# A hybrid convolution-attention block on one core: keys streamed once, the narrow band masked on GpSimd, products of ones on TensorE

## What is computed

```
# x: (8, 128, 16, 16)
attn = softmax(theta(x)^T phi(x), axis=1);  y = attn @ g(x);  x = w_mask y + x     # per image
t = tokens(x)                                                                      # (8, 256, 128)
# attention over 256 tokens, 8 heads of 16, in two bands
scores = q k^T * 16 ** -0.5
for ws in (9, 17):                       # half widths 4 and 8
    masked = where(|i - j| <= ws // 2, scores, -max)
    out += softmax(masked) @ v
t = t + (out / 2) @ proj_w.T + proj_b    # q, k, v from layernorm(t)
t = t + fp8(layernorm(t)) @ fp8(kernel) + bias
```

## Time and profile before

| | |
|---|---|
| Median of 3 runs | 106.75 us (106.66 to 107.17) |
| The profiled execution | 106.25 us, of which the span from first to last instruction is 104.5 us |
| PE busy | 87.1 us (83%), 1825 instructions |
| PE weight loads | 65.7 us (63%) |
| DVE busy | 77.4 us (74%), 283 instructions |
| ACT busy | 63.5 us (61%) |
| POOL busy | 56.3 us (54%) |
| Mean granted TensorE clock | 0.907 |

### The profile page before, as it was taken

One profiled execution on the slowest core, in us unless ns is written; L12 is line 12 of the kernel. 1 busy time (PEld: TensorE's weight loads), 2 busy tenths in 40 slices (PEclk: granted clock), 3 DMA queues, 4 the chain that ended last, 5 costly groups with the idle time before them and its releaser, 6 DMA issues.

```text
span 104.5 us, 4371 instructions
## 1 busy us (share of the span) xinstructions
PE 87.1 (83%) x1825; PEld 65.7 (63%) x1825; DVE 77.4 (74%) x283; ACT 63.5 (61%) x174; POOL 56.3 (54%) x118
## 2 busy tenths in 40 slices
PE   0799786999997999999999999989979757777260
PEld 0485474877775888797688788658849536444120
DVE  0011528199999999999999999999999895736221
ACT  1524556679584649974967956994996644162520
POOL 6810202057593944939799296789649464630300
PEclk9999999999999999999999999999999975555555
DMA  0725400000000000000010010000101010010101
GB/s 22 205 49 170 157 0 0 6 0 0 9 3 0 9 0 6 0 6 0 6 56 0 0 56 3 6 6 0 50 6 56 0 55 5 6 50 0 50 0 50
DMA packets 3971, 2.90 MB, mean 28 GB/s; under 512 B 944, under 2 KB 3952, under 8 KB 3952
## 3 DMA queue, kind: packets, MB, share of 16 engines
q1 hardware_dynamic: 3728, 2.56, 7.8%
q10 hardware_dynamic: 224, 0.07, 0.3%
HBM read 1.57 MB, written 1.05 MB: 25 GB/s over the span
## 4 chain that ended last, share of the span: by engine, by line
PE 55%; DVE 27%; POOL 8%; issue 3%; ACT 2%; DMA 2%; DVEq 0%
PE bank L309 10%; PE bank L323 5%; PE bank L331 5%; PE bank L300 4%; PE bank L257 4%; PE bank L266 4%; PE bank L252 4%; PE bank L274 3%; DVE row_max L791 3%; PE bank L293 3%; DVE z_sb L780 3%; PE bank L289 3%; DMA phi_w<-in_L_conv_w_phi_dram 2%; PE bank L272 2%; PE bank L294 2%
## 5 line engine op out<-in xcount | busy, mean ns | idle before, releaser
L309 PE MATMUL bank<-k_pad,q_four 64*64 64x64 f32 x512 | 17.4, 220 | 1.2 <-ACT q_four L548 1.1
L309 PEld LDWEIGHTS bank<-k_pad,q_four 64*64 64x64 f32 x512 | 15.8, 135 | 3.1 <-ACT q_four L548 1.8
L1122 POOL TENSOR_TENSOR prob<-expd,row_inv 128x256 f32<-128x256 f32 x16 | 9.9, 616 | 9.8 <-DVE row_inv L806 9.8
L323 PEld LDWEIGHTS bank<-prob_t,v_win 32*32 32x32 f32 x1024 | 10.9, 110 | 5.2 <-issue 2.7
L1116 POOL TENSOR_TENSOR diff<-narrow,row_max 128x192 f32<-128x192 f32 x16 | 8.2, 514 | 10.3 <-DVE row_max L791 10.3
L323 PE MATMUL bank<-prob_t,v_win 32*32 32x32 f32 x1024 | 12.7, 199 | 1.0 <-DVE prob_t L810 1.0
L548 ACT ACTIVATE q_four<-bank,four_mask 128x256 f32<-128x256 f32 x32 | 12.6, 483 | 0.0
L791 DVE TENSOR_REDUCE row_max<-bank 128x16 f32<-128x512 f32 x16 | 10.7, 671 | 2.1 <-ACT narrow L555 2.1
L1097 POOL TENSOR_TENSOR rstd<-ve,minus_half 128x2 f32<-128x2 f32 x8 | 5.6, 701 | 11.9 <-DVE ve L774 11.8
L555 ACT COPY narrow<-bank 128x192 f32<-128x192 f32 x16 | 5.1, 318 | 8.0 <-PE bank L309 8.0
L1129 POOL TENSOR_TENSOR prob<-prob,narrow_prob 128x192 f32<-128x192 f32 x16 | 9.5, 594 | 0.5
(11 more groups left out here) (116 smaller groups left out, 213.2 us busy)
## 6 DMA issues: line engine op xcount, KB each, us to landing
x_all<-in_x_dram SPq DMA_DIRECT2D x8, 128.0 KB, 3.8
out_dram<-out_all SPq DMA_DIRECT2D x8, 128.0 KB, 1.7
qkv_rows<-in_L_attn_qkv_w_dram SPq DMA_DIRECT2D x1, 192.0 KB, 2.6
proj_rows<-in_L_attn_proj_w_dram SPq DMA_DIRECT2D x1, 64.0 KB, 2.7
ffn_k<-in_L_ffn_kernel_dram SPq DMA_DIRECT2D x1, 64.0 KB, 2.2
proj_bias<-in_L_attn_proj_b_dram SPq DMA_DIRECT2D x1, 64.0 KB, 4.4
theta_w<-in_L_conv_w_theta_dram SPq DMA_DIRECT2D x1, 32.0 KB, 2.0
phi_w<-in_L_conv_w_phi_dram ACTq DMA_DIRECT2D x1, 32.0 KB, 2.4
```

Of the source, the lines that this page charges most:

```text
L309: last = mm(ps_scores[g][q, w, :, :], q_four[q, u % SLOTS, g * WB + w, :, :].rearrange("p e q -> p (e q)"), k_pad[q, u % SLOTS, at:at + KW ...
L323: last = mm(ps_pv[q, at:at + QUAD], v_win[q, u % SLOTS, g * WB + w, :], prob_t[q, u % SLOTS, g, w, :], start=True, stop=True)
L1122: p.tensor_tensor(prob[:, u % SLOTS, g], wide_part(expd, u, g), row_inv[:, u % SLOTS, g, 0].unsqueeze(2).to_broadcast([C, WB, KW]), ALU.mult)
```

## The change

It has five parts.

- The keys are streamed once: the score bank holds only the wide kind (256 columns instead of 512), the mask product has 256 columns, each score product 32.
- The narrow kind is made from the wide one: `copy_narrow` copies the inner 24 columns to a new tile `near`, `mask_narrow` on POOL adds a mask to it, and a new `narrow_max` on DVE takes its maximum; `band_max` reads 256 columns of PSUM. The narrow mask is spread over the 128 partitions once, by one small product (`spread_narrow`) and one copy.
- At the opening DVE fills a tile with ones, and PE makes 12 products of 256 columns in bfloat16 with it, ahead of its first product.
- In the last stretch nine groups of such products, 59 in all, stand in PE's list ahead of calls that wait. No one reads what they write.
- The lists of all four engines are written out in a new order.

```
+        warm_rows = sb("warm_rows", [C, TOK], BF16)
+            def keep_warm(at, count):
+                for _ in range(count):
+                    mm(bank[at][:, 0:TOK], warm_rows[:, 0:C], warm_rows[:, :], start=True, stop=True)
+
+            def begin_warm(count):
+                pe.wait_ge(warm_made, 1)
+                keep_warm(7, count)
+            def spread_narrow():
+                pe.wait_ge(masks_made, 1)
+                pe.wait_ge(weight_done, 3)
+                mm(bank[6][:, C:C + NW], query_sel[:, :, :].rearrange("p h q -> p (h q)"), narrow_rows[:, :],
+                   start=True, stop=True).then_inc(weight_mm, 1)
...
-                mm(bank[4 + g][:, :], query_sel[:, :, :].rearrange("p h q -> p (h q)"),
-                   key_mask[:, g:g + WB, :, :].rearrange("p w k n -> p (w k n)"), start=True, stop=False)
+                mm(bank[4 + g][:, 0:WB * KW], query_sel[:, :, :].rearrange("p h q -> p (h q)"),
+                   key_mask[:, g:g + WB, :].rearrange("p w n -> p (w n)"), start=True, stop=False)
...
-                        last = mm(ps_scores[g][q, w, :, :],
+                        last = mm(ps_scores[g][q, w, :],
                                   q_four[q, u % SLOTS, g * WB + w, :, :].rearrange("p e q -> p (e q)"),
-                                  k_pad[q, u % SLOTS, at:at + KW].unsqueeze(1).to_broadcast([SIDE, KINDS, KW]),
+                                  k_pad[q, u % SLOTS, at:at + KW],
...
+            begin_warm(12)
             fold_bilinear()
...
-                nc.scalar.copy(narrow[:, u % SLOTS, g], ps_scores[g][:, :, 1, INSET:INSET + NW]).then_inc(narrow_kept[g], 1)
+                nc.scalar.copy(near[:, u % SLOTS, g], ps_scores[g][:, :, INSET:INSET + NW]).then_inc(narrow_kept[g], 1)
...
-                v.tensor_reduce(row_max[:, u % SLOTS, g], ps_scores[g], AX.X, ALU.max).then_inc(max_done[g], 1)
+                v.tensor_reduce(row_max[:, u % SLOTS, g, 0], ps_scores[g], AX.X, ALU.max).then_inc(max_done[g], 1)
...
+            def narrow_max(u, g):
+                dve.wait_ge(narrow_made[g], u + 1)
+                v.tensor_reduce(row_max[:, u % SLOTS, g, 1], narrow[:, u % SLOTS, g], AX.X, ALU.max).then_inc(nmax_made[g], 1)
...
+            def mask_narrow(u, g):
+                if u == 0:
+                    pool.wait_ge(mask_kept, 1)
+                pool.wait_ge(narrow_kept[g], u + 1)
+                p.tensor_tensor(narrow[:, u % SLOTS, g], near[:, u % SLOTS, g],
+                                narrow_mask[:, :].unsqueeze(1).to_broadcast([C, WB, NW]), ALU.add).then_inc(narrow_made[g], 1)
...
             def subtract_narrow(u, g):
-                pool.wait_ge(max_done[g], u + 1)
+                pool.wait_ge(nmax_made[g], u + 1)
```

More of the change, by code:

```diff
@@ L151, in hybrid_block_kernel @@
         ps_q, ps_k = bank[3][:, 0:TOK], bank[3][:, TOK:2 * TOK]
-        ps_scores = [bank[4 + g][:, :].rearrange("p (w k n) -> p w k n", w=WB, k=KINDS) for g in range(BANKS)]
+        ps_scores = [bank[4 + g][:, 0:WB * KW].rearrange("p (w n) -> p w n", w=WB) for g in range(BANKS)]
         ps_pv, ps_proj = bank[6][:, :], bank[6][:, 0:TOK]
@@ L436, in _ @@
             turn_z2(1)
[L437 to L438 removed]
+            weigh_values(3, 0)
             project_kq(5)
[L440 to L441 removed]
             lay_mask(5, 0)
[L443 removed]
             feed_forward(1)
+            weigh_values(3, 1)
+            turn_t2(2)
             lay_mask(5, 1)
[L446 removed]
+            scores(5, 0)
+            project_g(7)
             scores(5, 1)
[L448 removed]
@@ L898, in _ @@
             row_inverse(1, 1)
+            window_values(2)
             band_max(2, 0)
-            norm_first(3)
-            pick_odd(0)
             turn_probs(1, 0)
-            window_values(2)
             residual(0)
+            band_max(2, 1)
+            stats_second(0)
+            narrow_max(2, 0)
+            subtract_max(2, 0)
+            stats_first(4)
+            column_max(5)
+            aggregate_first(4)
+            aggregate_second(0)
+            narrow_max(2, 1)
+            variance_first(4)
@@ L930, in _ @@
-            band_max(3, 1)
-            residual(1)
-            subtract_max(3, 1)
-            band_max(3, 0)
-            stats_first(5)
-            stats_second(1)
+            stats_first(5)
+            band_max(3, 1)
+            aggregate_second(1)
+            column_inverse(6)
+            band_max(3, 0)
+            subtract_max(3, 1)
+            quantise_half(0)
+            turn_probs(2, 1)
+            narrow_max(3, 0)
+            aggregate_first(5)
             subtract_max(3, 0)
-            turn_probs(2, 1)
@@ L972, in _ @@
-            pick_odd(3)
-            norm_first(6)
+            column_inverse(7)
             window_values(5)
-            column_inverse(7)
             turn_probs(4, 0)
-            band_max(5, 1)
-            residual(3)
-            band_max(5, 0)
-            subtract_max(5, 1)
-            subtract_max(5, 0)
-            turn_probs(4, 1)
-            stats_first(7)
+            residual(3)
+            narrow_max(5, 0)
+            band_max(5, 0)
+            stats_first(7)
+            subtract_max(5, 0)
@@ L993, in _ @@
             row_sums(5, 1)
-            pick_odd(4)
+            result(2)
             row_inverse(5, 1)
-            norm_first(7)
-            window_values(6)
-            result(2)
+            residual(4)
+            turn_probs(5, 0)
+            band_max(6, 1)
             band_max(6, 0)
-            band_max(6, 1)
-            turn_probs(5, 0)
+            subtract_max(6, 0)
+            turn_probs(5, 1)
+            narrow_max(6, 0)
+            quantise_tiny(3)
             subtract_max(6, 1)
-            residual(4)
@@ L1004, in _ @@
-            subtract_max(6, 0)
             stats_second(4)
-            quantise_tiny(3)
-            turn_probs(5, 1)
+            quantise_half(3)
+            aggregate_second(4)
+            narrow_max(6, 1)
+            variance_second(4)
+            result(3)
             row_sums(6, 0)
-            quantise_half(3)
+            pick_odd(5)
             row_inverse(6, 0)
             row_sums(6, 1)
-            aggregate_second(4)
             row_inverse(6, 1)
-            variance_second(4)
```

438 lines of the change are left out of this document (243 added, 195 removed).

## The result

The changed kernel takes 103.59 us (median of 4 runs, 103.46 to 106.99), the kernel before 106.85 (4 runs, 106.66 to 107.17); the ratio is 0.969, with a 95% interval of 0.966 to 0.972. The median is inside the stated range and 1.2 us above the predicted 102.4. The profiled execution takes 103.52 us with a span of 101.8. The fourth run left no trace; its mean granted clock of 0.983 says that its clock also fell somewhere behind the rise.

What follows compares the result with a forecast made beforehand. PE and DVE were taken as full together, PE deciding to 69 us, then DVE, then one chain at half clock. Terms −0.7 −0.8 −1.7 −1.0 = −4.2 us from 106.25 gave 102.05, stated as 102.4; eight in ten from 100.7 to 105.3.

Steps and rivals of the forecast that it cites:

- Scores, 0: PE's score products: halving streamed columns gains 0, as the 64-column weight load sets the pace; bounds 0 and 8 us.
- rival 4: The scores do halve, capped by DVE's remaining idle time: 1.3 us more gained, 101.1 us; chance 8%.
- Mask product, −1.0: PE's mask product loses 256 columns, 0.11 us each of 16 times; 1.0 us in reach where PE decides.
- Middle as a whole, −0.7: Middle stretch: −1.0 mask product, +0.1 `spread_narrow`, +0.2 DVE gives −0.7 us; range −2.0 to +1.5.
- DVE, +0.2: Two maxima on DVE replace one at 0.56 to 0.60 against 0.61 us; +0.2 us taken, at most 1.6 in all.
- POOL, 0: 16 new `mask_narrow` on POOL, 8.2 to 9.5 us, and a longer narrow path, hidden by other units' work: cost 0.
- rival 2: The longer narrow path stalls DVE, half the units waiting 0.6 us each: 2.4 us come back, 104.8 us; chance 17%.
- Opening, −0.8: Twelve products raise PE's clock well before 10 us: 1.4 us won, 0.6 lost; bounds +0.6 and −1.6.
- rival 3: The opening's products don't bring the clock sooner: +0.6 in place of −0.8 us, 103.8 us; chance 12%.
- Drain, clock, −1.7: Products of ones hold PE at full clock in the drain, shortening the last chain by 1.7 us.
- Drain, order, −1.0: New order for the last unit: 0.7 and 0.6 us won, 0.3 off for stalls; bounds 0 and −2.0.
- Rival 1: The higher clock is lost in the drain despite the products: 1.7 us gain becomes 3.2 loss, 107.3 us; chance 8%.

Runs made afterwards that it cites:

- both sets: The kernel before with 12 products of ones at the opening and 50 late ones, nothing else; six runs from 103.78 to 106.32 us, ratio 0.977.
- narrow loads: The changed kernel with 32 instead of 64 weight columns in seven of eight score windows, half the heads' scores left out there; 102.65 and 103.14 us.
- the kernel with one exponential: The changed kernel with one subtraction and exponential for both bands, narrow probabilities cut out by a mask on POOL, lists otherwise unchanged; 125.84 us, ratio 1.165.

## Why the prediction was right, and where its sum was off

The forecast was faster by 4.2 us in the profiled execution; 2.7 came, within the range. The direction and the two clocks were right as mechanisms; every term but the two zeros was mis-sized, the order of the drain most. Step by step:

- *Scores, 0*: right, and shown from both sides: twice the streamed columns cost 0.02 us a unit, half the loaded columns bring the products of one half of the array from some 62 to 33 ns. The rule of the Trainium skill's page "TensorE: Matmul & The Clock Gate" (section "LDWEIGHTS (loading the stationary operand)") held against the view that streamed columns set the time, and rival 4 is out.
- *Mask product, −1.0*: some 0.6 to 0.75. At the start of the last bank's scores the new kernel is 0.80 us ahead, counted from the first scores (60.23 against 61.03 us), and with the wide mask product put back it is 0.06 ahead (60.97). So this relief of PE arrived, and the rest of the band and the order changed nothing up to there.
- *Middle as a whole, −0.7*: −0.10. What is lost is lost behind that point: from the start of the last bank's scores to the end of its subtraction pass 6.06 us before and 6.76 now. In the kernel before `project(5)` stands ahead of `scores(7, 1)` in PE's list (79.75 us in the earlier trace rows); now it stands behind, and DVE waits for it:

```profile
80.29 1.15 PE L309 MATMUL bank<-k_pad,q_four 64*64 64x64 f32 x32
```

```profile
78.08 1.12 PE L331 MATMUL bank<-k_pad,q_four 64*64 64x32 f32 x32
79.14 0.71 PE L353 MATMUL bank<-proj_t,att_t 128*128 128x128 f32 x4
79.95 0.42 DVE L867 TENSOR_TENSOR t_sb<-bank,tb_all 128x256 f32<-128x256 f32 x1 [0.67 <-PE bank L353]
```

The wait of 0.67 us is about what is lost, but no run moved that one call, so it is the likely cause, not shown. Taking the masking out (0.17) or three other residuals behind ready calls (0.21) shortens only what lies ahead: from the last bank's scores on it stays 6.76 us in both.
- *DVE, +0.2*: not seen. DVE's busy time fell from 77.4 to 75.6 us; in a full queue the two maxima take 0.32 and 0.24 us of the chain, against 0.61 for the one.
- *POOL, 0* was right, and rival 2 is out, though POOL has 15 of 16 us in one stretch. Full is not the same as deciding. From 31 to 69 us it is at 29.1 of 38 us, 76% and not the 86% of the forecast. The sign that was to refute the forecast, DVE waiting for `narrow`, did appear, once and for 0.31 us.
- *Opening, −0.8*: −1.41, of which 1.33 come with the products alone. The sum took 1.4 us won and 0.6 lost; PE began its first real product at 3.92 instead of 3.22 us, so 0.7 was lost and 2.1 won, since the clock was up before the first product of 256 columns. What was not foreseen is that it is a draw: rival 3 happens in part of the executions, and then the scores start 1.3 us later than in the kernel before, where it had 0.6, and 2.6 us later than in a good execution.
- *Drain, clock, −1.7*: −1.15, by the products alone in the old order.
- *Drain, order, −1.0*: 0. The drain is 14.82 us with the new order and 14.85 with the old.

The last two can be taken apart with the chains of the three kernels, unit 7, bank 1 (us):

| | before | late products, old order | changed |
|---|---|---|---|
| last subtraction's end to `scale_probs` | 3.29 | 3.14 | 2.44 |
| to `project` | 4.54 | 4.52 | 4.13 |
| to `residual` | 1.33 | 0.82 | 1.73 |
| to the last result's end | 6.84 | 6.37 | 6.52 |
| sum | 16.00 | 14.85 | 14.82 |

The first two columns are the clock. The projection gave 0.51 of the forecast's 0.61. Behind the residual 0.47 came where 0.75 was forecast: of the feed-forward only some 0.2 is on the chain, as its second product waits for ACT's copy, and the first of the two transposes gave nothing, as POOL's `rstd_second` takes as long beside it (2.85 us from the residual to `norm_second` before, 2.82 with the products). The 0.3 for the last values did not come at all (4.54 to 4.52): there too the chain goes through POOL and ACT, not through PE.

The last two columns are the order. Up to the projection it won 0.70 and 0.39 us, the 1.0 of the forecast. Then 0.91 went again at `residual(7)`: it stands behind `quantise_tiny(6)` in DVE's list, which waits 1.45 us for a transpose (92.80), while its own input is there from 92.12. Three products of ones stand in that chain too, from 92.12 to 92.44; the transpose's input is there at 92.27, so they cost 0.2 us where the forecast had 0. I took turns that a call gives up as time won, without following the calls that stand behind it to the end.

Of the 2.7 us, the products bring 2.5 (1.33 and 1.15) in executions in which both work, the band and the order some 0.2.

That the time lies in the range is in part luck. The opening's 0.6 us more stands against 2.1 us less in the other terms. And the median is that of a good draw: three of four executions had the short opening, where the same twelve products gave a short time in two of four and two of six executions of the old order. With an opening as in the profiled execution that missed, the changed kernel would take some 106.1 us (103.5 + 2.6, an estimate), outside the range and 0.7 us from the kernel before.

Rival 1 (the clock lost in the drain) did not come in the changed kernel's trace, but it was nearer than thought: without the late products the clock falls one to five microseconds earlier in the new order than before (84 and 80 us against 85). With them it fell near 80 us in two variants' traces, just ahead of the first group, and from 89 to 93 us, amid the groups, in a third.

## What to carry to other kernels

Before you shorten what a product streams, look at what its weight load takes: if the load lasts as long, a shorter stream gives nothing, and a widened copy of the kernel shows it in one run. Products without a reader in a late wait are cheap, and here the clock stayed up from 86 us to the last result in eight of ten traces with them, where it was down in all four without; at an opening they are a draw, so look at every run's time and not at the ratio alone. And a term that says "this call now stands in a gap" needs the whole list behind it read to the end: here what it won was lost again a few calls later.

## What the runs showed of the hardware

- The granted clock's rise at the opening isn't fixed by the program. The twelve products end at 4.0 us in all four of these: a product of 256 columns takes 0.70 us at 4.81 us in the changed kernel, and 1.22 us at 5.06 and 9.26 in the one without late products, whose list is the same up to 79 us; 0.70 us at 5.00 with the opening's products in the kernel before, and 1.22 us at 5.07 and 9.48 with both sets. The first scores start 2.6 us apart in each pair.
- The clock can fall in a busy stretch and return: from 81 to 84 us without the opening's products, from 79 to 86 with 18 of them, from 52 to 55 with narrow loads. PE was busy for 4.3, 4.3 and 4.2 of the 5 us ahead. In the changed kernel it was busy for 4.3 of the 5 us from 75 to 80 us, with the same list, and the clock stayed. The page's line of clocks shows falls and returns most of all in the kernel with one exponential, whose PE waits often:

```profile
PEclk9999999998699999658976995599997569995999
```

- Products of 64x32 in f32 on the two halves of the array follow each other by the load: 64 loaded columns take 1.99 to 2.08 us for 64 records whether 32 or 64 columns are streamed; with 32 loaded columns 28 records start within 0.44 us.
